# Deformable layer on one Trainium2 core: corner weights and the upper five window rows of the dense taps kept in PSUM

## What is computed

```python
offset = _conv2d(x, w_p, b_p, padding=1)
m = jax.nn.sigmoid(_conv2d(x, w_m, b_m, padding=1))
...
x_off = g_lt[:, None] * gather(q_lt_x, q_lt_y) + g_rb[:, None] * gather(q_rb_x, q_rb_y) + g_lb[:, None] * gather(q_lt_x, q_rb_y) + g_rt[:, None] * gather(q_rb_x, q_lt_y)
x_off = x_off * jnp.transpose(m, (0, 2, 3, 1))[:, None]
...
return _conv2d(x_off, w_conv, None, stride=KS, padding=0)
```

## Time and profile before

| what | value |
|---|---|
| time, median of 3 runs | 536.98 us (535.08 to 537.48) |
| the profiled execution, its own time | 537.87 us |
| its span, first to last instruction | 535.2 us |
| granted TensorE clock, mean | 0.925 of full speed |
| busy in the span: PE, DVE, POOL, ACT | 468.0, 389.7, 332.7, 148.6 us |
| second layer's gathers: first issue, last issue | 191.47 us, 524.53 us |

### The profile page before, as it was taken

How to read it: one execution, slowest core, us unless ns; L and a number is a source line. 1 busy time by engine, 2 the same in 40 slices (tenths; PEclk the granted TensorE clock), 3 DMA queues, 4 the chain that set the end, 5 groups by cost and what they waited for, 6 DMA issues and landing times.

```text
span 535.2 us, 10660 instructions
## 1 busy us (share of the span) xinstructions
PE 468.0 (87%) x3862; PEld 263.4 (49%) x3862; DVE 389.7 (73%) x876; ACT 148.6 (28%) x292; POOL 332.7 (62%) x336
## 2 busy tenths in 40 slices
PE   3688698989964978999999998999998999998794
PEld 3346264547543724555555554455444544544443
DVE  2556367687955458988987986898787888888682
ACT  3311120111123623234334333143231333232211
POOL 2167356565500057777777777777777777777772
PEclk9956798988995959999999999899998999999989
DMA  4899669577700784222322329212212212212211
GB/s 114 235 238 212 158 158 203 105 127 131 142 4 9 216 227 98 69 54 74 91 73 69 91 75 130 60 45 56 56 53 57 55 53 57 55 55 55 60 50 32
DMA packets 41924, 52.23 MB, mean 98 GB/s; under 512 B 16767, under 2 KB 32931, under 8 KB 41873
## 3 DMA queue, kind: packets, MB, share of 16 engines
q1 hardware_dynamic: 31464, 30.19, 25.9%
q0 software_dynamic: 10240, 20.99, 15.2%
q10 hardware_dynamic: 168, 0.34, 0.2%
HBM read 34.80 MB, written 8.72 MB: 81 GB/s over the span
## 4 chain that ended last, share of the span: by engine, by line
PE 42%; POOL 21%; issue 13%; DMA 8%; DVE 7%; SPq 5%; ACT 2%; POOLq 0%; DVEq 0%; ACTq 0%
POOL got L614 21%; PE ps_later L1178 5%; PE ps_pair L1178 5%; PE ps_raw L980 4%; PE ps_x L1192 4%; PE ps_raw L1152 3%; PE ps_pair L1045 3%; DMA xn<-xq 3%; DMA got<-table,idx 3%; SPq L478 3%; PE ps_x L1045 2%; PE ps_x L1202 2%; DMA shared<-positions 2%; PE ps_o L993 2%; DVE samples L1803 1%
## 5 line engine op out<-in xcount | busy, mean ns | idle before, releaser
L614 POOL DMA_INDIRECT got<-table,idx x320 | 325.5, 1017 | 141.2 <-issue 92.8
L1820 DVE TENSOR_TENSOR prod<-got,wgt 128x512 f32<-128x512 f32 x64 | 44.1, 689 | 31.3 <-DMA got<-table,idx 31.3
L1621 DVE TENSOR_TENSOR vprod<-ps_pair,rhat 128x704 f32<-128x704 f32 x64 | 56.6, 885 | 5.0 <-PE ps_pair L1178 4.3
L1803 DVE TENSOR_TENSOR samples<-shared,vprod 128x800 f32<-128x800 f32 x48 | 47.2, 986 | 17.1 <-PE ps_x L1045 11.8
L1192 PEld LDWEIGHTS ps_x<-early,vprod 128*128 128x128 f32 x384 | 42.4, 145 | 29.9 <-issue 18.2
L1192 PE MATMUL ps_x<-early,vprod 128*128 128x128 f32 x384 | 56.2, 283 | 0.6 <-DVE vprod L1629 0.4
L1621 DVE TENSOR_TENSOR vprod<-ps_later,rhat 128x704 f32<-128x704 f32 x64 | 56.4, 881 | 0.3 <-PE ps_later L1178 0.3
L1629 DVE TENSOR_TENSOR vprod<-vprod 128x640 f32<-128x640 f32 x64 | 53.0, 828 | 1.2
L1202 PE MATMUL ps_x<-early,prod 128*128 128x128 f32 x256 | 39.1, 275 | 9.9 <-DVE prod L1820 9.9
L1152 PE MATMUL ps_raw<-conv_out,later 128*128 128x512 f32 x64 | 38.5, 685 | 0.7 <-ACT shared L834 0.7
L980 PE MATMUL ps_raw<-xn,early 128*32 128x512 f32 (+1 forms) x128 | 27.0, 852 | 13.1 <-DMA xn<-xq 9.5
(11 more groups left out here) (216 smaller groups left out, 683.5 us busy)
## 6 DMA issues: line engine op xcount, KB each, us to landing
shared<-positions SPq DMA_DIRECT2D x24, 440.0 KB, 9.1
xn<-xq SPq DMA_DIRECT2D x52, 132.0 KB, 3.8
got<-table,idx POOLq DMA_INDIRECT x320, 7.4
table<-trow SPq DMA_DIRECT2D x9, 234.0 KB
table<-trow SPq DMA_DIRECT2D x2, 1024.0 KB, 5.1
out<-ysumT SPq DMA_DIRECT2D x64, 16.0 KB
columns_of<-table SPq DMA_DIRECT2D x2, 512.0 KB, 8.3
table<-trow SPq DMA_DIRECT2D x1, 936.0 KB
```

Of the source, the lines that this page charges most:

```text
L614: pool.indirect_dma_start(into[t][:, s * P:(s + 1) * P], None, tab, bass.IndirectOffsetOnAxis(ap=idx[:, slot, k:k + 1], axis=0),).then_inc ...
L1621: nc.vector.tensor_tensor(dst, ps_dense[pair_number(0, t, pair) % 2][:].rearrange("p (d n) -> p d n", d=2)[:, :, 0:WROWS * C].rearrange("p ...
L1803: nc.vector.tensor_tensor(wprod[t % 2].rearrange("p (y x c) -> p y x c", y=SIDE, c=C), window[n // TT % NWIN][:, :, 2 * t * C:(2 * t + SID ...
L1820: nc.vector.tensor_tensor(prod[:, t % 2, :].rearrange("p (k s c) -> p s k c", k=CORNERS, c=C), got[t].rearrange("p (s k c) -> p s k c", s= ...
```

## The change

The diff, cut to what matters (`ps_x[1]` is one bank of 512 columns):

```diff
+CORN1 = TT * GT * CORNERS
+        ps_turned = ps_x[0]
+        ps_upper = ps_x[1][:, 0:2 * (WROWS - HALF) * C].rearrange("p (d w c) -> p d w c", d=2, c=C)
+        wgt1 = ps_x[1][:, GPIX - 2 * CORN1:GPIX].rearrange("p (u n) -> p u n", u=2)
...
-            return 6 * g + sum(2 - k % 2 for k in range(t + 1))
+            return PAIRS * g + sum(3 - k % 2 for k in range(t + 1))
...
-                bank = ps_x[t % 2]
+                bank = ps_turned
                 pe.wait_ge(v_added, additions_done(tile // TT, t))
-                if tile >= 2:
-                    pe.wait_ge(trans_copied, tile - 1)
+                if tile >= 1:
+                    pe.wait_ge(trans_copied, tile)
...
-                        wgt[:, u, 0:4 * N].rearrange("p (n y x) -> p n y x", y=2, x=2),
+                        wgt1[:, u, :].rearrange("p (n y x) -> p n y x", y=2, x=2),
...
                     if pair < 2:
...
+                        def multiply(into, a, z):
+                            return nc.vector.tensor_tensor(into, dense[:, :, a:z, :], hats_of[:, :, a:z, :], ALU.mult)
+                        if pair == 0:
+                            if not (first and t == 0):
+                                dve.wait_ge(v_added, additions_done(g, t - 1))
+                            multiply(ps_upper, HALF, WROWS)
+                            multiply(rows[:, :, 0:HALF, :], 0, HALF).then_inc(v_read, 1)
+                        else:
+                            multiply(rows[:, :, 0:HALF, :], 0, HALF)
+                            dve.wait_ge(v_added, additions_done(g, t - 1) + 1)
+                            multiply(ps_upper, HALF, WROWS).then_inc(v_read, 1)
+                        between(pair)
+                        dve.wait_ge(v_read, n + 1)
+                        lower = rows[:, :, 0:WROWS - HALF, :]
+                        nc.vector.tensor_tensor(lower, lower, ps_upper, ALU.add).then_inc(v_added, 1)
...
-                dve.wait_ge(v_read, pairs_done(g, t))
-                half = WROWS - HALF
-                nc.vector.tensor_tensor(vprod[:, t % 2, 0:half, :], vprod[:, t % 2, 0:half, :],
-                                        vprod[:, t % 2, HALF:WROWS, :], ALU.add).then_inc(v_added, 1)
...
-                    wgt[:, u, 4 * GT * t:4 * GT * (t + 1)].rearrange("p (s k) -> p s k", s=GT).unsqueeze(3).broadcast_to(
+                    wgt1[:, u, 4 * GT * t:4 * GT * (t + 1)].rearrange("p (s k) -> p s k", s=GT).unsqueeze(3).broadcast_to(
...
-            corner_weights(1, 0, NI, usual)
             row_weights(0)
             for k in range(2, TT):
                 copy_columns(k)
+            corner_weights(1, 0, NI, usual)
```

More of the change, by code:

```diff
@@ L820, in copy_samples @@
                 nc.scalar.activation(samples[u][:, :, t * P:(t + 1) * P],
-                                     ps_x[t % 2][:, 0:BLOCKS1 * P].rearrange("p (k n) -> p k n", k=BLOCKS1),
+                                     ps_turned[:, 0:BLOCKS1 * P].rearrange("p (k n) -> p k n", k=BLOCKS1),
                                      ACT.Copy).then_inc(trans_copied, 1)
@@ L1487, in corner_weights @@
                 link(nc.vector.tensor_tensor(rw, rw, m.unsqueeze(3).broadcast_to([P, TT, S, 2]), ALU.mult))
-                link(nc.vector.tensor_tensor(wgt[:, slot, 0:4 * N].rearrange("p (n y x) -> p n y x", y=2, x=2),
+                made = wgt1[:, slot, :] if l == 1 and taps is None else wgt[:, slot, 0:4 * N]
+                link(nc.vector.tensor_tensor(made.rearrange("p (n y x) -> p n y x", y=2, x=2),
                                              fr[:, 0:N, :].unsqueeze(3).broadcast_to([P, N, 2, 2]),
@@ L1615, in weigh_rows @@
                     dve.wait_ge(v_mm, n + 1)
+                    dense = ps_dense[pair_number(0, t, pair) % 2][:].rearrange("p (d n) -> p d n", d=2)[
+                        :, :, 0:WROWS * C].rearrange("p d (w c) -> p d w c", c=C)
                     if pair < 2:
-                        dst = vprod[:, t % 2].rearrange("p w (d c) -> p d w c", c=C)[:, 2 * pair:2 * pair + 2]
-                        hats_of = rhat[:, u, t * DT + 2 * pair:t * DT + 2 * pair + 2, :]
-                    else:
-                        dst, hats_of = vlast[:], rhat[:, u, t * DT + 4:(t + 1) * DT + 5:DT, :]
@@ L1621, in weigh_rows @@
-                    nc.vector.tensor_tensor(
-                        dst,
-                        ps_dense[pair_number(0, t, pair) % 2][:].rearrange("p (d n) -> p d n", d=2)[
-                            :, :, 0:WROWS * C].rearrange("p d (w c) -> p d w c", c=C),
-                        hats_of.unsqueeze(3).broadcast_to([P, 2, WROWS, C]), ALU.mult).then_inc(v_read, 1)
-                    between(pair)
-                dve.wait_ge(v_read, pairs_done(g, t))
-                half = WROWS - HALF
@@ L1629, in weigh_rows @@
-                nc.vector.tensor_tensor(vprod[:, t % 2, 0:half, :], vprod[:, t % 2, 0:half, :],
-                                        vprod[:, t % 2, HALF:WROWS, :], ALU.add).then_inc(v_added, 1)
+                        rows = vprod[:, t % 2].rearrange("p w (d c) -> p d w c", c=C)[:, 2 * pair:2 * pair + 2]
+                        hats_of = rhat[:, u, t * DT + 2 * pair:t * DT + 2 * pair + 2, :].unsqueeze(3).broadcast_to(
+                            [P, 2, WROWS, C])
+                        def multiply(into, a, z):
+                            return nc.vector.tensor_tensor(into, dense[:, :, a:z, :], hats_of[:, :, a:z, :], ALU.mult)
@@ new lines, in weigh_rows @@
+                        between(pair)
+                        dve.wait_ge(v_read, n + 1)
+                        lower = rows[:, :, 0:WROWS - HALF, :]
+                        nc.vector.tensor_tensor(lower, lower, ps_upper, ALU.add).then_inc(v_added, 1)
+                    else:
+                        hats_of = rhat[:, u, t * DT + 4:(t + 1) * DT + 5:DT, :].unsqueeze(3).broadcast_to([P, 2, WROWS, C])
+                        nc.vector.tensor_tensor(vlast[:], dense, hats_of, ALU.mult).then_inc(v_read, 1)
+                        between(pair)
@@ L1631, in weigh_rows @@
                 if t % 2 == 0:
+                    dve.wait_ge(v_read, pairs_done(g, t))
                     nc.vector.tensor_tensor(vlast[:, :, 0:WROWS - KEPT, :], vlast[:, :, 0:WROWS - KEPT, :],
```

## The result

The changed kernel took 522.68 us, the median of 4 runs (519.89 to 524.78). The kernel before took 537.23 us on the same chip (4 runs, 535.08 to 537.55). The ratio is 0.9711 with a 95% interval of 0.9667 to 0.9756, so the change saves 2.9%, or 15.5 us (13.1 to 17.9). The forecast was 526.0 us in a range of 522 to 534 us. The mechanism was right; one term of the sum was too small, and the spread of the second layer's start was not in the sum at all.

A forecast was written before the change was run, and what follows sets the result against it. The prediction took POOL's 256 gather issues with their gaps, plus a tail, as the bound; removing 11.9 us of stretch (8.8 + 3.1) from the profiled 537.87 us, other costs taken as hidden, gave 526.0 us, range 522 to 534.

The forecast's parts named there:

- The 11.9 us under L1629 and L1820: POOL's gather issues: stretch of 8.8 us under L1629 and 3.1 under L1820 goes once each reads one input from PSUM.
- The other 2.8 us stay: POOL's 18 issues stretched under shorter two-SBUF-input DVE instructions keep their loss of about 2.8 us.
- upper bound of 14.7 us: Largest gain on POOL's issues, if the 2.8 us under short instructions vanish too; the lower bound was 9.1 us.
- The low end of the range: Forecast time of 522 us, taking in that the median lies 0.9 us below the profiled execution.
- DVE's extra work: DVE's split multiplications and additions: busy time rises from 16.9 to 17.7 to 18.7 us a group, 13 to 28 overall.
- A PSUM output and PSUM inputs: DVE's rows on PSUM: same price as SBUF; otherwise 2.7 us a group for writes, 0.8 us for inputs.
- The additions' place: DVE's additions of pairs 0 and 1 fall into pair 2's waits of 1.7 and 1.2 us; PE keeps its pace.
- PE and DVE follow POOL: Second layer: some 6.3 us behind POOL at tile 24, they gain 1.28 us a group and are level after five.
- DVE and PE falling short: Rival, chance 0.15: PE waits up to 0.55 us a tile for pair 1's bank; 529 to 534 us.
- PSUM as the second operand not freeing POOL: Rival, chance 0.10: operand order decides, so additions still stretch issues, 6.6 us in place of 8.8; about 535.7 us.
- DVE as the bound: Rival, chance 0.07: multiplications into PSUM at twice the time a column, 21.4 us a group, end at 555 us.
- the 20.33 of the prediction: DVE's group time in us, from its prods between 207.0 and 527.2 us, above which the kernel becomes slower.

The follow-up runs named there:

- new order in SBUF: The changed kernel with the upper rows and corner weights both in SBUF instead of PSUM, only addresses differing; 534.43 us, ratio 0.9873 to the kernel before.
- second profile: The changed kernel run once more, unedited, for a closer interval and another trace; 525.77 us, ratio 0.968 to the kernel before.
- weights alone: The kernel before with only the corner weights in PSUM, plus the single transpose bank and moved first weights; 536.1 us, ratio 0.9875.
- bank and order only: The kernel before with only one bank for all transposes and the first group's corner weights moved; 538.15 us, ratio 0.9988.
- PSUM first: The changed kernel with the PSUM operand as first input of the additions and of `prod`; 525.14 us, ratio 0.9762 to the kernel before.
- upper rows alone: The changed kernel with only the corner weights back in SBUF, upper rows still in PSUM; 529.89 us, ratio 0.9848 to the kernel before.
- 4 more rows on DVE: The changed kernel with one unread 320-column multiplication more per tile, 4 a group; 523.20 us in one run.

## Why the prediction was right, and where it was wrong

**The bound and the mechanism: right.** The time is the sum of 256 issues and their gaps, and what stretches an issue is a DVE instruction with two SBUF inputs. The new order in SBUF and the change have the same instructions, and differ by 12.7 us on POOL (333.1 and 320.4). The 11.9 us under L1629 and L1820 went to the last tenth. The Trainium skill, page "SBUF — State Buffer", section "Who interferes with whom", says that a DVE instruction with two SBUF inputs contends with a GpSimd instruction that reads SBUF, and that one with at most one, outside of the modes that use two ports, does not; the trace agrees, with 1.39 us under L1629 and 0.94 us under L1621. Its inference that `tensor_tensor` leaves descriptor generation alone is not borne out for these issues: 59 of 256 are held in the new order in SBUF and cost 12.1 us.

**The step that failed: "The other 2.8 us stay, since the short instructions still have two SBUF inputs."** They fell to 0.8 us, and to 1.0 us in the second profile. The short rows were still there, but of these 2.8 us 1.7 lay under L1588, and seven of its eight held issues followed a hold by L1629, as shown above. So the term is 13.1 to 13.9 us and not 11.9. The prediction had an upper bound of 14.7 us for it, and this took that case in, but as a chance of POOL's phase and not as something that hangs on the term beside it.

What made the loss smaller is in part open, since the change did two things at once: it took the long holds away, and it gave the `rhat` row another place, 0.78 us behind an addition of 320 columns where it had been 2.34 us behind L1629. Where the additions stay as they were (weights alone, bank and order only) 11 and 9 issues are held under that row, 7 and 4 of them in the way shown; in the change, its repeat and the run with PSUM first 1 or 2. But the new order in SBUF has 45 holds by additions and none under the `rhat` row, so there the new place alone was enough. In six of the 14 groups the row starts just as a held issue ends, as in these two rows:

```profile
278.58 1.27 POOL L619 DMA_INDIRECT got<-table,idx  x1 [0.30 <-issue]
```
```profile
279.81 0.38 DVE L1594 TENSOR_TENSOR rhat<-rdist,mod 128x220 f32<-128x220 f32 x1
```

The upper rows alone have the new place too and 5 holds under that row. Four of them follow a hold by `prod`, and the row starts 1.44 to 1.52 us after the held issue's end, as it did behind L1629 in the kernel before (301.41 - 299.89 = 1.52). One of them (DVE's rows, then POOL's):

```profile
274.84 0.68 DVE L1838 TENSOR_TENSOR prod<-got,wgt 128x512 f32<-128x512 f32 x1
...
277.87 0.38 DVE L1594 TENSOR_TENSOR rhat<-rdist,mod 128x220 f32<-128x220 f32 x1
```
```profile
275.35 0.99 POOL L619 DMA_INDIRECT got<-table,idx  x1 [0.30 <-issue]
276.65 0.95 POOL L619 DMA_INDIRECT got<-table,idx  x1 [0.30 <-issue]
277.90 1.16 POOL L619 DMA_INDIRECT got<-table,idx  x1 [0.31 <-issue]
```

And with 4 more rows on DVE four issues are held there with no hold just ahead, and short rows cost 1.9 us. So the loss under short rows depends on both the holds and the places of the rows, and it is no fixed sum.

**The low end of the range.** 537.87 - 14.7 = 523.2 us, and 0.9 us for the median made 522. It left out that the first gather is issued anywhere from 187.5 to 191.7 us. With the measured 13.9 us in place of 11.9 the same sum gives 523.1 us, still inside the range: the larger term alone doesn't explain a time below 522. In the first profile of the change 13.9 of its 18.0 us (537.87 - 519.89) come from POOL, 3.5 from the earlier start, 0.1 from the tail and 0.5 from the time around the span (2.6 us before, 2.1 after); in the second, which is 13.1 us shorter, POOL's 256 issues are 13.1 us shorter (334.3 - 321.2). The measured 15.5 us (13.1 to 17.9) hold POOL's gain, and the 1.6 to 2.4 us above it can't be told from this spread.

**DVE's extra work: right.** 13.2 us more were busy, against 13 to 28. The windows of three groups (length, busy time of each engine, PEclk, DMA share, GB/s), which answer to the earlier trace rows:

```profile
278.98:298.71 19.73, 19.73 (x192) 10.81 (x191) 17.78 (x50) 7.37 (x15) 14.93 (x16) 1.00 0.29 82
319.16:337.43 18.27, 18.27 (x185) 10.09 (x184) 17.72 (x49) 6.21 (x13) 13.88 (x15) 1.00 0.73 100
394.85:414.67 19.82, 19.02 (x188) 9.81 (x184) 17.84 (x50) 6.05 (x13) 14.94 (x17) 1.00 0.20 57
```

DVE is busy 17.7 to 17.9 us in each, at the lower end of 17.7 to 18.7. The first is still paced by PE, busy 19.73 of 19.73 us; the second catches up with POOL, in 18.27 us; in the third PE has time to spare, since POOL sets the pace with 16 issues in 19.82 us.

**A PSUM output and PSUM inputs: right.** 320 columns into PSUM take 492 ns, 384 columns into SBUF 549 (550 were predicted), and an addition of 320 columns with one PSUM input 482, where L1755 took 483. `prod` takes 682 ns, 4 less than before. The 62 cycles for an input from PSUM, which the prediction took as an estimate from the Trainium skill (page "VectorE: DVE Perf Modes", section on the TRN2 errata), don't show in these rows.

**The additions' place: right.** Pair 2's two multiplications now wait 1.26 and 0.66 us for PE, in the rows below, where they waited 1.7 and 1.2:

```profile
308.14 0.89 DVE L1646 TENSOR_TENSOR vlast<-ps_later,rhat 128x704 f32<-128x704 f32 x1 [1.26 <-PE ps_later L1183]
...
297.51 0.89 DVE L1646 TENSOR_TENSOR vlast<-ps_pair,rhat 128x704 f32<-128x704 f32 x1 [0.66 <-PE ps_pair L1183]
```

**PE and DVE follow POOL: right, and sooner.** Tile 24 is weighed at 319.16 us and its last gather is issued at 311.79 us. With 2.6 us to land, DVE is some 4.8 us behind. The prediction's 6.3 us took the end of that issue for its start; counted as here it would have been 7.5. The next three groups take 18.27, 18.94 and 18.28 us, to 374.65 us, and the first wait of `prod` for a gather ends one tile later, in the fourth group and not after five. That row, and then the first of DVE's waits from 200 to 510 us:

```profile
380.41 0.69 DVE L1838 TENSOR_TENSOR prod<-got,ps_x 128x512 f32<-128x512 f32 x1 [1.62 <-DMA got<-table,idx]
```
```profile
DVE prod L1838 <- DMA got<-table,idx: 16.9, 17, 3.0
```

**The rivals.** DVE and PE falling short: not seen; PE's groups from 319.16 us on are 18.3 to 18.9 us long until POOL paces them. PSUM as the second operand not freeing POOL: fell, by no issue held under additions or `prod` in the change and in the run with PSUM first; where short additions do hold, in the new order in SBUF, they cost 8.6 us and not the 6.6 that this rival was priced at. DVE as the bound: not seen. DVE is busy 17.8 us in a group, 2.5 us short of the 20.33 of the prediction; it took 8 rows of 0.49 us more in a group until it set the pace.

## What to carry to other kernels

Before an engine's time is cut, see whether its instructions have one length: here 63 of 256 were longer than the rest, and the row on another engine under which they began was the cause, with the number of its SBUF inputs as what told them apart. Moving one input of such a row into PSUM paid here although it cost its own engine 13.2 us, because that engine's time for a group, 17.8 us, stayed below the pace of 19.96. And stretches on a paced engine are linked: a held instruction is released at a fixed time after the row that held it, so that the loss under one row can't be priced apart from the others: the weights alone lost under the additions what they had won under `prod`, and the whole change won more than the two rows that it was made for.

## What the runs showed of the hardware that was not expected

The instruction that holds an issue is the one in flight at its start, and the hold ends with it: 0.43 us left give 0.31 us of stretch, 0.57 give 0.45, 0.34 give 0.22, each time 0.12 us less. In the eleven traces 411 issues are longer than 0.97 us. For 400 of them what was left of the row, less the stretch, is 0.11 to 0.14 us; the other 11 are the first issue of each trace. A further row with two SBUF inputs that begins under the same issue adds nothing: the 1.39 us issue of the earlier trace rows runs on under L1632, with two inputs too, and is no longer than L1629 makes it.

A row that has only just begun is itself the one that waits. Here an issue starts 0.03 us into L1629, in the kernel before:

```profile
356.88 0.89 DVE L1629 TENSOR_TENSOR vprod<-vprod 128x640 f32<-128x640 f32 x1
356.91 0.94 POOL L614 DMA_INDIRECT got<-table,idx  x1 [0.30 <-issue]
```

The issue keeps its 0.94 us, and L1629 takes 0.89 us where its median is 0.825. Six issues under L1629 and two under L1820 start like this in the kernel before, 0.00 to 0.04 us into the row; none is stretched, and all eight rows are longer than their median, by 0.04 to 0.08 us.

Two tiles in SBUF as inputs are also not the only thing that holds an issue. With 4 more rows on DVE three issues that start under L1570, which reads one tile, are held by about 0.09 us, each with 0.22 us of the row left. One of them (DVE's row, then POOL's):

```profile
390.21 0.26 DVE L1570 TENSOR_SCALAR rdist<-rdist 128x220 f32<-128x220 f32 x1
```
```profile
390.25 1.03 POOL L619 DMA_INDIRECT got<-table,idx  x1 [0.30 <-issue]
```

Because a hold ends with its row, an issue and the rows of DVE are in a fixed phase after each hold, and a short row at the right distance, 2.34 us behind L1629 here, is met time after time.
